# A 16-head attention rebuilt as a one-layer stream, and a stream's lead-in that offers only batch 0's chains

## What is computed

```python
def _L3_attn_ref(x, Wq, bq, Wk, bk, Wv, bv, Wo, bo):     # 16 heads of 8
    q_mat = split_heads(x @ Wq.T + bq)
    k_mat = split_heads(x @ Wv.T + bv)
    v_mat = split_heads(x @ Wk.T + bk)
    q_mat, k_mat = _xpos_rotate(q_mat, k_mat)            # q*cos*scale + rotate_half(q)*sin*scale
    ...                                                  # causal softmax(q k^T) v
h = _layernorm(x, axis=-1) * (1 + ca) + sa
x = x + ga * _L3_attn_ref(h, ...)
```

## Time and profile before

| | |
|---|---|
| median of three runs | 3065.41 us |
| the profiled execution | 3066.68 us |
| its span (first to last instruction) | 3064.4 us |
| TensorE (matmul) busy | 2492.6 us, 81% |
| VectorE busy | 1859.1 us, 61% |
| ScalarE busy | 1401.8 us, 46% |
| GpSimd busy | 518.4 us, 17% |
| mean granted TensorE clock | 0.871 of 2.4 GHz |

### The profile page before, as it was taken

The page is one execution under the profiler, slowest core; times in us unless marked ns, Lnnn a source line. Parts: engine busy times, 40 slices in busy tenths (PEclk is TensorE's granted clock), DMA queues, the critical chain, the costliest instruction groups (busy, mean ns, idle before and its releaser), DMA issues. The chain is left out here.

```text
span 3064.4 us, 38232 instructions
## 1 busy us (share of the span) xinstructions
PE 2492.6 (81%) x12636; PEld 1027.0 (34%) x12636; DVE 1859.1 (61%) x4326; ACT 1401.8 (46%) x2451; POOL 518.4 (17%) x582
## 2 busy tenths in 40 slices
PE   6789989999989999998669796974566985888848
PEld 4323333333433433333233322431123331333325
DVE  3576676666676766766145675358997255666242
ACT  3255565555665656665335133354232431656320
POOL 1200111010111111100009100007892000000000
PEclk7589899899998999999769898987898985999968
DMA  2211112121122112121010000004331022010020
GB/s 86 91 48 51 67 67 73 57 82 53 59 78 74 65 62 81 49 77 39 15 33 1 20 1 25 0 12 144 124 142 57 1 64 66 32 36 18 15 84 14
DMA packets 74145, 165.39 MB, mean 54 GB/s; under 512 B 19954, under 2 KB 35698, under 8 KB 70262
## 3 DMA queue, kind: packets, MB, share of 16 engines
q1 hardware_dynamic: 73948, 162.95, 15.3%
HBM read 126.51 MB, written 35.39 MB: 53 GB/s over the span
## 5 line engine op out<-in xcount | busy, mean ns | idle before, releaser
L1503 ACT ACTIVATE sb_prob<-ps 128x512 f32<-128x512 f32 (+1 forms) x1216 | 650.5, 575 | 463.2 <-PE ps L1314 311.5
L1288 PE MATMUL ps<-sb_k_stack_half,sb_q_stack_half 78*128 78x512 bf16 (+3 forms) x1536 | 486.3, 350 | 57.4 <-DMA sb_q_stack_half<-alibi 30.2
L1314 PE MATMUL ps<-sb_q_stack_half,sb_k_stack_half 81*128 81x512 bf16 (+2 forms) x1792 | 474.5, 322 | 51.1 <-ACT sb_prob L1503 49.3
L1424 DVE TENSOR_REDUCE sb_row_max<-ps 128x1 f32<-128x512 f32 x512 | 346.3, 686 | 158.5 <-PE ps L1288 157.4
L1433 DVE CUSTOM_DVE_ANT_0 sb_masked_scores<-ps,sb_mask_row,sb_row_max 128x128 bf16<-128x128 f32 (+3 forms) x512 | 273.6, 544 | 94.3 <-PE ps L1288 91.5
L1433 DVE CUSTOM_DVE_ANT_0 sb_masked_scores<-ps,sb_mask_row 128x128 bf16<-128x128 f32 (+3 forms) x512 | 228.6, 488 | 156.4 <-PE ps L1288 155.8
L1314 PEld LDWEIGHTS ps<-sb_q_stack_half,sb_k_stack_half 81*128 81x128 bf16 x1792 | 165.7, 101 | 330.3 <-ACT sb_prob L1503 157.4
L1335 PE MATMUL ps<-sb_prob,sb_v_first_half 128*9 128x512 f32 (+3 forms) x2048 | 255.9, 575 | 0.0
L688 DVE CUSTOM_DVE_ANT_0 sb_masked_scores<-ps,sb_mask_row 128x128 f32<-128x128 f32 (+7 forms) x256 | 183.8, 756 | 107.7 <-PE ps L617 106.2
L2682 PE MATMUL ps<-sb_read_out,sb_ident 128*128 128x512 f32 x256 | 139.1, 676 | 120.5 <-DVE sb_read_out L2769 114.6
L1288 PEld LDWEIGHTS ps<-sb_k_stack_half,sb_q_stack_half 78*128 78x128 bf16 x1536 | 152.7, 103 | 228.3 <-DVE sb_row_max L1433 61.8
(11 more groups left out here) (400 smaller groups left out, 3831.6 us busy)
## 6 DMA issues: line engine op xcount, KB each, us to landing
sb_q_stack_half<-q_rows SPq DMA_DIRECT2D x192, 96.0 KB
sb_k_stack_half<-k_rows SPq DMA_DIRECT2D x96, 192.0 KB
o_rows<-sb_o_raw SPq DMA_DIRECT2D x64, 256.0 KB, 3.9
sb_b_spread<-b_rows SPq DMA_DIRECT2D x32, 512.0 KB, 4.7
sb_c_spread<-c_rows SPq DMA_DIRECT2D x32, 512.0 KB, 3.4
sb_k_stack_half<-k_rows SPq DMA_DIRECT2D x96, 96.0 KB
q_rows<-sb_qk_parts SPq DMA_DIRECT2D x48, 128.0 KB, 2.7
k_rows<-sb_qk_parts SPq DMA_DIRECT2D x48, 128.0 KB, 2.1
```

Source lines behind the costliest of these rows:

```text
L1288: pe.matmul(M.ps[:, k % RING, 0:hi - lo], qst[half][0:S1_ROWS, s, j, at:at + P], kst[half][0:S1_ROWS, s, lo // CH, j, 0:hi - lo], start=Tr ...
L1314: mm = pe.matmul(bank[:, x * w + lo:x * w + hi], kst[half][0:S2_ROWS, s, t // 4, j, t % 4 * P:(t % 4 + 1) * P], qst[half][0:S2_ROWS, s, j, ...
L1424: dve.reduce_max(rowmax[:, tau % 3, 0, at:at + 1], M.ps[:, k % RING, 0:w], AX_X).then_inc(first_done, 1)
L1503: act.activation(prob[:, st % PROB_STEPS, heads[0]:heads[-1] + 1, a:CH], scores.rearrange("p (j q) -> p j q", j=len(heads)), ACT.Exp).then ...
```

## The change

`attn_l3` no longer uses `qkv`, `attention_core` and `attention_out`, which are deleted together with the `Attention` class and the constants `pick_sums`, `unpick_sums` and `k_aux`. It calls `decoder`, which takes a `Form`: for level 0 four layers with the feed-forward part and without rotation, for level 3 one layer without it, with rotation, a gain and its own loads. In a rotating form a chain has q0, q, k0, k, v: q0 is the matmul by the plain weights with its table on VectorE (into `turn_a`), q that by the swapped weights (into `turn_b`), followed on VectorE by the addition of both. The projection with a gain is one VectorE operation and an addition on GpSimd. The chain's layer norm is the one of the stream, so level 3's own `layer_norm` phase goes too. `wo` shrinks from 512 columns to 128.

In both streams the lead-in's steps without first pieces end when chunk 0's chain is laid, and until the first weighing only chunks 0 and 1 are offered. GpSimd's `norm` stands ahead of the side piece of its step. All the rest of level 0's plan follows from these rules.

```diff
-    def __init__(self, layers):
-        self.layers = layers
+    def __init__(self, layers, ffn, rotate):
+        self.layers, self.ffn, self.rotate = layers, ffn, rotate
...
+        if beta and not self.ffn:
+            return [("proj", 0.0)]
         if beta:
             out += [("proj", 0.0), ("mean", 2.0), ("var", 3.2), ("bcast", 3.4), ("up0", 3.6), ("up1", 0.0),
                     ("up2", 0.0), ("up3", 0.0), ("down0", 7.0), ("down1", 0.0)]
         if beta < self.layers:
-            out += [("mean", 2.0), ("var", 3.2), ("bcast", 3.4), ("q", 3.6), ("k", 0.0), ("v", 0.0)]
+            out += [("mean", 2.0), ("var", 3.2), ("bcast", 3.4)]
+            out += ([("q0", 3.6), ("q", 0.0), ("k0", 0.0), ("k", 0.0), ("v", 0.0)] if self.rotate else
+                    [("q", 3.6), ("k", 0.0), ("v", 0.0)])
         return out
 
...
+            if name in ("q0", "k0"):
+                return turn_of is None
             return True
 
         def choose(now):
-            for q in range(NQ):
+            for q in range(NQ if weighing else 2):
                 if ready[q] is not None and at[q] < len(items[q]) and ready[q] <= now and allowed(q, items[q][at[q]][0]):
                     return q
             return None
...
+            if self.rotate and name in ("q0", "q", "k0", "k"):
+                turn_of = q if name[1:] else None
...
-        while any(at[q] < len(items[q]) for q in (0, 1)):
+        while at[0] < len(items[0]):
...
         done = 0.0
+        weighing = True
         for st, (tau, t) in enumerate(steps):
...
-
-
-    plan = Plan(LAYERS)
+class Form:
+
+
+    def __init__(self, layers, ffn, rotate, alibi, col, weights_at, affine, gain=None, tables=None, loads=()):
+        self.layers, self.ffn, self.rotate, self.alibi, self.col = layers, ffn, rotate, alibi, col
+        self.weights_at, self.affine, self.gain, self.tables, self.loads = weights_at, affine, gain, tables, loads
+
+
+def decoder(nc, M, D, F, W=None):
+
+
+    plan = Plan(F.layers, F.ffn, F.rotate)
+    col = F.col
     steps, tasks = plan.steps, plan.tasks
     S2_BANK, RING, O_BANK, SIDE = 3, 3, 6, 7
     ROWS = 4 * GROUP
...
-                            pe.matmul(out, col(l, "w" + name), h_of(n), start=True, stop=True).then_inc(side_ready, 1)
+                            which = "w" + name[0] + ("r" if F.rotate and name[1:] != "0" else "")
+                            pe.matmul(out, col(l, which), h_of(n), start=True, stop=True).then_inc(side_ready, 1)
...
-                    if name == "proj":
+                    if name == "proj" and F.gain:
+                        if q >= 6:
+                            dve.wait_ge(x_added, q - 5)
+                        dve.tensor_scalar(update[:, q % 2, :], ps, col(l - 1, "bo"), F.gain(q // 2 % 2), ALU.add,
+                                          ALU.mult).then_inc(side_free, 1)
+                    elif name == "proj":
...
+                    elif name in ("q0", "k0"):
+                        if plan.turns_of[(name, q)]:
+                            dve.wait_ge(rotated, plan.turns_of[(name, q)])
+                        dve.scalar_tensor_tensor(turn_a[:], ps, col(l, "b" + name[0]), F.tables(name[0], q % 2)[0], ALU.add,
+                                                 ALU.mult).then_inc(side_free, 1)
+                    elif F.rotate:
+                        u = plan.part_of[(name, q)]
+                        if u >= 2:
+                            dve.wait_ge(lo_ready, u - 1)
+                        if u:
+                            dve.wait_ge(rotated, u)
+                        dve.scalar_tensor_tensor(turn_b[:], ps, col(l, "b" + name + "r"), F.tables(name, q % 2)[1], ALU.add,
+                                                 ALU.mult).then_inc(side_free, 1)
+                        dve.wait_ge(side_free, m + 1)
+                        dve.tensor_tensor(full[:, u % 2, :], turn_a[:], turn_b[:], ALU.add).then_inc(rotated, 1)
...
                         u = plan.part_of[(name, q)]
+                        if F.rotate:
+                            act.wait_ge(rotated, u + 1)
                         act.wait_ge(side_free, m + 1)
...
-                    if name == "var":
+                    if name == "proj" and F.gain:
+                        pool.wait_ge(side_free, m + 1)
+                        pool.tensor_tensor(z(q), z(q), update[:, q % 2, :], ALU.add).then_inc(x_added, 1)
+                    elif name == "var":
...
                     before = None
+                    for c in plan.norm_at.get(s, ()):
+                        norm(c)
                     if step["side"]:
                         side(*step["side"], step["m"])
                         before = (*step["side"], step["m"])
-                    for c in plan.norm_at.get(s, ()):
-                        norm(c)
...
     L3_COLS[_name] = (_at, _at + _w)
     _at += _w
@@ -2074,21 +1645,21 @@
 
     with ExitStack() as ctx:
         W = ctx.enter_context(sbuf(nc, "l3_weights", [P, L3_WIDTH]))
-        A = Attention(nc, D, ctx)
-        with ExitStack() as tmp:
-            xpos = tmp.enter_context(sbuf(nc, "xpos", [P, 4, T]))
-            layer_norm(nc, M, M.x, M.h, lambda b: M.mod[:, 3, 1, b:b + 1], lambda b: M.mod[:, 3, 0, b:b + 1],
-                       [(W[:], D["l3_weights"]), (xpos[:].rearrange("p k t -> p (k t)"), D["xpos"])] + A.loads)
-
-            def tables(what, c):
-                t = slice((c % 2) * CH, (c % 2 + 1) * CH)
-                return xpos[:, 2 * what, t], xpos[:, 2 * what + 1, t]
-
-            qkv(nc, M, A, W, L3_COLS, 1.0, tables)
-        attention_core(nc, M, A, [D["no_bias"].rearrange("r (j t) -> r j t", j=GROUP)] * NGRP)
-        a, b = L3_COLS["wo"]
-        o = L3_COLS["bo"]
-        attention_out(nc, M, A, W[:, a:b], W[:, o[0]:o[1]], M.x, lambda b: M.mod[:, 3, 2, b:b + 1])
+        xpos = ctx.enter_context(sbuf(nc, "xpos", [P, 4, T]))
+
+        def col(l, name):
+            a, b = L3_COLS[name]
+            return W[:, a:b]
+
+        def tables(what, c):
+            t = slice(c * CH, (c + 1) * CH)
+            k = 0 if what == "q" else 2
+            return xpos[:, k, t], xpos[:, k + 1, t]
+
+        loads = [(W[:], D["l3_weights"]), (xpos[:].rearrange("p k t -> p (k t)"), D["xpos"])]
+        decoder(nc, M, D, Form(1, False, True, [D["no_bias"]] * NGRP, col, lambda l: 16 * len(loads),
+                               lambda l, ln, b: (M.mod[:, 3, 0, b:b + 1], M.mod[:, 3, 1, b:b + 1]),
+                               lambda b: M.mod[:, 3, 2, b:b + 1], tables, loads))
 
 
```

More of the change, by code:

```diff
@@ L900, in lay_steps @@
         means = vars_ = bcasts = 0
-        ffn_of = None
+        ffn_of = turn_of = None
         half_down = None
+        weighing = False
         def allowed(q, name):
@@ L923, in take @@
         def take(q, end):
[L924 removed]
+            nonlocal means, vars_, bcasts, ffn_of, half_down, turn_of
             name = items[q][at[q]][0]
@@ L1631, in transformer @@
                    [(fin[:], D["l0_final"]), (W[:, 0, :], D["l0_weights"][0:P, :])])
-        decoder(nc, M, D, W, [D["alibi"][g * 6:g * 6 + 6] for g in range(NGRP)])
+        def col(l, name):
+            a, b = L0_COLS[name]
+            return W[:, l % 2, a:b]
+        decoder(nc, M, D, Form(LAYERS, True, False, [D["alibi"][g * 6:g * 6 + 6] for g in range(NGRP)], col,
+                               lambda l: 16 * l, lambda l, ln, b: (col(l, ln + "b"), col(l, ln + "w"))), W)
         with ExitStack() as tmp:
```

478 lines of the change are left out of this document (24 added, 454 removed).

## The result

The change takes 3036.78 us (median of four runs, 3033.16 to 3038.86) against 3066.03 before (four runs, 3064.05 to 3070.88), a ratio of 0.990 (95% interval 0.988 to 0.992). Measured again beside the kernel before on another chip it was 3036.25 against 3066.93, 0.990 (0.987 to 0.993). That is 29 us, where 25 were forecast.

The account below looks back on a forecast made before the run. The stream was taken to be paced by its steps, TensorE first, VectorE near behind. Level 0 -3.9, level 3 -24.7 and the next layer norm +3.6 sum to -25.0: 3066.7 to 3041.7, forecast 3041 us, range 3021 to 3062.

Parts of the forecast that it names:

- Level 3's lead-in and tail: Level 3 before first weighing and after last save: lead-in 36.4 us shorter, tail 23.3 shorter.
- Level 0's lead-in: Level 0 before its first weighing: weighing starts at 103.1 us, 18.2 earlier, including 1.3 added for row maxima.
- Level 0's moved pieces: Eleven pieces moved into the weighing of level 0's tasks 0 to 2 cost 1.3 us each, 14.3 in all.
- Slower, SyncE's queue: Rival, chance 0.07: late parts on SyncE delay stacks behind them, four waits of 9.76 us, +39, total 3080.
- two steps to be made: Argument against late parts on SyncE: the plan gives a part two steps, and a stack 16 us of lead.
- Level 0: -3.9: Level 0's sum: lead-in -18.2 us plus moved pieces +14.3 gives -3.9.
- Level 3's batch 0: Level 3's first weighing batch: 181.6 + 15 x 1.3 - 14 x 1.0 = 187.1 us.
- Level 3's batch 1: Level 3's second weighing batch: 149.0 less 22 pieces at 1.0 us gives 127.0.
- The layer norm ahead of moe_l3: After level 3's tail, TensorE restarts at low clock: norm takes 22.0 us instead of 18.4, +3.6.
- Wash: Rival, chance 0.12 with the lead-in rival: 26 moved pieces cost 2.1 us, not 1.3, +21, total 3062.
- clock gains: Rival, chance 0.14: moved pieces fill TensorE at batch starts, up to 20 us of low clock may not recur, 3021.
- doesn't shorten: Rival, counted in the wash's 0.12: first weighing waits behind stacks on SyncE, level 0 at +14, total 3059.

Follow-up runs that it names:

- Run 4: The change with parts of chunks 2 and 3 in level 0's first layer issued four steps later on SyncE: 3023.66 us, 0.987 of the kernel before.
- run 2: The kernel before, with its old level 3 attention, plus only the new lead-in in level 0: 3067.68 us, ratio 1.0027.
- run 3: The change, but with level 0's lead-in by the old rule, so the new lead-in in level 3 alone: 3034.35 us, 0.991 of the kernel before.
- run 1: The change, level 3 as a stream, but both lead-ins by the old rule: 3038.27 us, 0.992 of the kernel before.
- run 10: The change itself, unaltered, again on another chip beside the kernel before: 3036.25 us, ratio 0.990.
- run 6: The kernel before with four stack slots for half 1 instead of three: 3043.65 us, ratio 0.992.
- run 5: The change with four stack slots for half 1 instead of three (the slot): 2979.85 us, 0.973 of the kernel before.
- run 7: The change with four stack slots for half 1 and the old lead-in rule in both streams: 2979.63 us, 0.972 of the kernel before.

## Why the prediction was right, and which steps weren't

The direction, the size (29 for 25) and the large terms were right. Level 3's lead-in and tail are worth 64.2 us (forecast 59.7), and the stream's own weighing gives back 30.1 (forecast 35.0). Level 3 as a whole came out 34.1 us shorter where 24.7 was forecast. That the total came so close is partly luck: the start of level 0 was 12.0 us worse than forecast (+8.1 for -3.9), level 3 was 9.4 better, and the stretches that I had put at nothing moved by -8.2 and +7.4.

- **Level 0's lead-in: right in time, wrong in its worth.** -16.2 for -18.2. The 1.3 us I added for row maxima behind stack 3 was too little, since TensorE waited 5.29 us for them. In level 3 it was the other way round: the 4.5 us that I put there for the same reason did not come, no wait stands ahead of 2558.76, and the lead-in lost 41.3 us for 36.4.
- **Level 0's moved pieces: the step that failed.** "11 x 1.3 = 14.3" was +24.3 in the profile. Run 4 splits it: 8.2 us for the pieces themselves, 0.75 each and so below even my lower end of 1.0, and 16 us for waits behind SyncE's queue and the clock that they cost. The rival "Slower, SyncE's queue" is the mechanism, with its place as written (parts of chunks 2 and 3 between stacks 5 and 6). It came at 1.7 to 5.3 us a wait in level 0 and 2.55 in level 3 instead of 9.8. The plan's "two steps to be made", my argument against it, doesn't hold: chunk 3's k was ready 8.7 us after SyncE had come to it. So "Level 0: -3.9" should have been +8, as the segments of three profiles against three show and run 2 measured by itself, though the ratio of run 3 doesn't bear it out.
- **The profile hid it.** Level 0 ended 0.3 us earlier than before, for its other seven batches took 8.2 us less. That was no effect of the change: the old plan took 1177.6 to 1191.1 us for them in three profiles (before, runs 1 and 3), the new one 1180.7 to 1187.8 (the change, runs 2 and 10).
- **Level 3's batch 0: 174.8 for 187.1.** The same price, 15 x 1.3 = 19.5, was too dear. Tasks 0 to 3 took 67.6 us against 59.5 with one piece, 0.54 each, with none of the waits; against level 3's own tasks in run 1, 60.1 with 5 pieces, it is 0.68 each. The subtraction at 1.0 each for tasks 4 to 7 held: 107.2 us against 302.93 - 180.78 = 122.2 for 14 pieces less. It is again partly luck, since 6.5 of the 107.2 us are task 4's wait and clock. Why a piece costs more late in a batch wasn't tried.
- **Level 3's batch 1: 134.4 for 127.0.** I forgot the wait for task 7's stack here. With few pieces TensorE comes to it early, and it costs 9.53 us (layer 3's batch 1 in level 0 had only 4.16). With the slot it took 119.7. The sum also starts from a wrong count: the prediction gives that batch 24 pieces, with a down half counted as one, and its trace shows 20. By that count the same sum is 149.0 - 18 = 131.0.
- **The layer norm ahead of moe_l3: wrong sign.** Its first four matmuls took 3.75 us, as forecast from the earlier trace rows, but then the clock rose and it lasted 15.4 us instead of 22.0. In nine of the twelve profiles, two with the old tail among them, it lasted 15.2 to 15.4, in the others 18.4 (before), 19.4 (run 1) and 21.9 (run 10, the change itself). The row of 22.0 was one draw, and so was the agreement with the Trainium skill ("TensorE: Matmul & The Clock Gate", "HAM oscillation — how this bites in real kernels") that I read into it. The cold start of the clock is there (3.75), its price is under 2 us. And the tail is not what makes it: with the old tail the four matmuls took 3.59 and 3.60 us in runs 2 and 6, and the 1.96 of the profile before was the exception.
- **Wash, clock gains and "doesn't shorten".** "Doesn't shorten" fell. The wash fell as a mechanism; that level 0's 11 pieces came to 24.3 us, 2.2 each, is its number by way of the waits. The clock gains were real where I looked for them. Level 0's task 0 was granted 0.71 in all five profiles with the old lead-in and took 24.0 to 24.6 us with one piece; with four pieces it was granted 0.82 to 0.88 in all seven with the new one and took 22.9 to 24.2. Level 3's tasks 1 to 3 were granted 1.00 in the profile after. In level 0 the waits took it back: task 4 was granted 0.80.

Open: whether the new lead-in in level 3 is worth anything. It cost 1.6 us with three slots (run 1 against the change) and gained 3.1 with four (run 5 against 7), both about as large as what a segment repeats to. Without task 4's wait it would gain some 6 us more, an estimate from 28.0 against 21.5; no run removes that wait without making another.
